# Three 16-head attentions: sums of the exponentials halved on GpSimd, two heads of each wave taken by ACT from PSUM

## The reference

```python
q = split_heads(queries @ Wq + bq)            # 8 x 16 x 128 x 8
k = split_heads(keys @ Wk + bk)
v = split_heads(values @ Wv + bv)
scores = jnp.einsum('bhqd,bhkd->bhqk', q, k) / jnp.sqrt(jnp.float32(HD))
scores = jnp.where(mask, jnp.float32(-1000000000000000.0), scores)
attn = jax.nn.softmax(scores, axis=-1)
ctx = jnp.einsum('bhqk,bhkd->bhqd', attn, v)
return ctx @ Wo + bo
```

## Time and profile before

| | us |
|---|---|
| median of 3 runs | 948.28 (948.22 to 954.27) |
| the profiled execution, span | 948.7 |
| PE busy | 882.5 (93%) |
| DVE busy | 670.6 (71%) |
| ACT busy | 556.3 (59%) |
| POOL busy | 182.2 (19%) |
| line 777 on DVE (128x512, PSUM and SBUF in), 192 times | 132.5, mean 690 ns |

### The profile page before, as it was taken

How to read it: one execution, slowest core, us unless ns; L and a number is a source line. 1 busy time by engine, 2 the same in 40 slices (tenths; PEclk the granted TensorE clock), 3 DMA queues, 4 the chain that set the end, 5 groups by cost and what they waited for, 6 DMA issues and landing times.

```text
span 948.7 us, 15321 instructions
## 1 busy us (share of the span) xinstructions
PE 882.5 (93%) x5199; PEld 572.2 (60%) x5219; DVE 670.6 (71%) x1123; ACT 556.3 (59%) x963; POOL 182.2 (19%) x157
## 2 busy tenths in 40 slices
PE   8999998999789888989899988999999999999997
PEld 4576645666535543445545554676446888888885
DVE  4566627777778849658858845542347999999996
ACT  5356624555655547366656541232476888888886
POOL 0111012332000000000020006335100443334430
PEclk9999999999999999999999999999999999999999
DMA  9000001111000000000000052401106999999982
GB/s 358 10 1 0 0 1 34 34 33 64 1 1 2 1 1 1 0 1 1 2 1 2 1 210 74 135 23 52 61 1 156 243 242 239 233 242 245 239 226 67
DMA packets 27746, 76.76 MB, mean 81 GB/s; under 512 B 4464, under 2 KB 10864, under 8 KB 27264
## 3 DMA queue, kind: packets, MB, share of 16 engines
q1 hardware_dynamic: 26448, 73.50, 28.2%
q0 software_dynamic: 1248, 2.57, 0.8%
HBM read 72.31 MB, written 5.27 MB: 82 GB/s over the span
## 4 chain that ended last, share of the span: by engine, by line
PE 69%; DVE 17%; ACT 9%; issue 3%; DMA 1%; SPq 0%; POOL 0%; DVEq 0%; another core or an unknown queue 0%; ACTq 0%; POOLq 0%
PE ps L743 9%; PE ps L745 9%; PE ps L744 9%; PE ps L1106 4%; PE ps L582 3%; PE ps L574 3%; PE ps L1122 2%; PE ps L599 2%; PE ps L593 2%; PE ps L280 2%; DVE arena L712 2%; PE ps L1386 2%; PE ps L217 2%; DVE arena L716 2%; DVE parts L777 2%
## 5 line engine op out<-in xcount | busy, mean ns | idle before, releaser
L743 PE MATMUL ps<-parts 128*128 128x512 f32 x416 | 169.0, 406 | 7.0 <-DVE parts L957 3.4
L745 PE MATMUL ps<-parts 128*128 128x512 f32 x416 | 162.3, 390 | 0.0
L744 PE MATMUL ps<-parts 128*128 128x512 f32 x416 | 162.2, 390 | 0.0
L773 ACT ACTIVATE parts<-ps 128x512 fp32r<-128x512 f32 x192 | 115.1, 600 | 61.2 <-PE ps L745 32.9
L777 DVE TENSOR_TENSOR parts<-ps,parts 128x512 fp32r<-128x512 f32 x192 | 132.5, 690 | 7.2 <-ACT parts L773 1.5
L2394 DVE TENSOR_TENSOR ps<-ps,arena 128x512 f32<-128x512 f32 x156 | 108.3, 694 | 3.6 <-DMA arena<-m_comb 2.5
L743 PEld LDWEIGHTS ps<-parts 128*128 128x128 f32 x416 | 78.2, 188 | 36.7 <-DVE parts L777 9.7
L1930 ACT ACTIVATE ps<-ps 128x512 f32<-128x512 f32 x156 | 90.8, 582 | 2.9 <-PE ps L745 0.4
L761 POOL TENSOR_TENSOR parts<-ring,zeros 128x1024 fp32r<-128x1024 f32 (+2 forms) x36 | 50.8, 1421 | 214.3 <-PE ps L745 177.3
L745 PEld LDWEIGHTS ps<-parts 128*128 128x128 f32 x416 | 78.1, 188 | 16.7
L744 PEld LDWEIGHTS ps<-parts 128*128 128x128 f32 x416 | 78.2, 188 | 15.2 <-issue 0.5
(11 more groups left out here) (447 smaller groups left out, 1402.0 us busy)
## 6 DMA issues: line engine op xcount, KB each, us to landing
arena<-m_comb SPq DMA_DIRECT2D x156, 256.0 KB, 5.6
ring<-m_in SPq DMA_DIRECT2D x20, 512.0 KB
arena<-m_in SPq DMA_DIRECT2D x4, 1408.0 KB
pack<-pack_in SPq DMA_DIRECT2D x1, 2058.5 KB, 10.2
ring<-m_up_in SPq DMA_DIRECT2D x8, 256.0 KB
slots_x<-empty_in SPq DMA_DIRECT2D x1, 1491.6 KB
pack<-pack_in SPq DMA_DIRECT2D x1, 1186.0 KB, 14.7
pack<-pack_in SPq DMA_DIRECT2D x1, 1149.5 KB, 12.3
```

Source lines behind the costliest of these rows:

```text
L743: nc.tensor.matmul(dst, w_high, x_high, start=start, stop=False, skip_group_check=True)
L744: nc.tensor.matmul(dst, w_high, x_low, start=False, stop=False, skip_group_check=True)
L745: return nc.tensor.matmul(dst, w_low, x_high, start=False, stop=stop, skip_group_check=True)
L773: nc.scalar.activation(m_hh[0:rows, p], ps[0:rows, src, :], ACT.Copy).then_inc(R(t, "_hh"), 1)
```

## The change

For the first seven elements the sums no longer come from PE. POOL adds the halves of each exponential row three times (128 columns to 64, 32 and 16) for six of the eight heads of a wave, DVE sums the 16 that are left, takes the reciprocals of the 16 sums of an element (one per query and head) and copies each to 8 columns; PE transposes that 128x128 tile (`turn_inverse`), ACT copies it to SBUF (`spread_inverse`), and DVE's `outputs` only multiplies. The last element keeps `total` and the reciprocal.

The other two heads of a wave (`DIRECT`) are not subtracted by DVE: ACT reads their scores from PSUM, with the negated maximum as bias, and gives their sums by `accum_out`. So the subtraction and the exponential in place cover 768 columns, and the scores of the next wave in the same banks wait for the exponentials. The scale 8^-0.5 moves to q: to the activation that adds q's bias (with the bias scaled ahead), and in f2 to the products with cosine and sine.

```diff
--- before.py
+++ after.py
@@ -28,6 +28,7 @@
 NH, HD = 16, 8
 ROWG = 4
 GH = NH // ROWG
+DIRECT = 2
 XH = 8
 E = 8
 NE, TOPK = 160, 8
@@ -326,8 +328,14 @@
         a_p = A(8192, 2, NH // 2, P)
         a_q = A(10240, T)
         a_k = A(11264, T)
-        a_mx = A(12288, 2, NH // 2)
+        a_nmx = A(12288, 2, NH // 2)
         a_rec = A(12304, 2, P)
+        a_sum = A(12560, 2, 2, NH // 2)
+        a_inv = A(20352, 2, P)
+        a_one = A(12592, NH)
+        a_half = A(20864, NH // 2 - DIRECT, HD * 8)
+        a_quarter = A(21376, NH // 2 - DIRECT, HD * 4)
+        a_eighth = A(21632, 2, 2, NH // 2 - DIRECT, HD * 2)
         a_v = A(12672, B, NH, 4 * HD)
         a_vflat = A(12672, B * NH * 4 * HD)
         a_rope = A(16768, 2, 2, 2, HALF)
...
@@ -496,8 +505,8 @@
 
         WAVES, UNITS = 2 * B, (E * 2 * M0_CH, NB)
         LEFT = {"a_kproj": 2, "a_qproj": 2, "a_q_ready": 2, "a_k_ready": 2, "a_kb0": GH, "a_kb1": GH, "a_vproj": 1, "a_v_ready": 1,
-                "a_scores": WAVES, "a_mx": WAVES, "a_z": WAVES, "a_p": WAVES, "a_turned": WAVES, 
-                "a_pt": WAVES, "a_weighed": B, "a_rec": B, "a_oT": B, "a_rope_k": 0, "a_rope_q": 0,
+                "a_scores": WAVES, "a_mx": WAVES, "a_z": WAVES, "a_p": 2 * WAVES, "a_turned": WAVES, 
+                "a_pt": WAVES, "a_added": 3 * (WAVES - 2), "a_weighed": B, "a_rec": B, "a_spread": B - 1, "a_oT": B, "a_rope_k": 0, "a_rope_q": 0,
                 "m_logits": 1, "m_lg": 1, "m_e": 1, "m_pad": (1, B + 1), "m_parts": (3, 4), "m_wturned": 1, "m_wT": 1, "m_spread": (2 * E, 2 + NB - SOON), "m_xw": (2 * E, NB),
                 "m_xwh": (2 * E, NB), "m_xwl": (2 * E, 2 + NB - SOON),
                 "m_xh": 2, "m_xl": 2, "m_wh": (2 * E, 2), "m_split": (E, 1),
@@ -576,7 +585,7 @@
                 ins.then_inc(R(t, "_scores"), 1)
 
             def turn(v, w):
-                wait("_p", w + 1)
+                wait("_p", 2 * w + 2)
                 wait("_pt", w)
                 for n in range(NH // 2):
                     ins = nc.tensor.transpose(ps[:, 4 + n // 4, (n % 4) * P:(n % 4 + 1) * P], a_p[:, v, n, :], ident)
...
@@ -600,6 +609,11 @@
                                  a_pt[:, b % 2, r * GH + n, :], start=(n == 0), stop=(n == GH - 1), skip_group_check=True,
                                  tile_position=(0, 32 * r))
                 ins.then_inc(R(t, "_weighed"), 1)
+
+            def turn_inverse(b):
+
+                wait("_rec", b + 1)
+                nc.tensor.transpose(ps[:, 6 + b % 2, P:2 * P], a_inv[:, b % 2, :], ident).then_inc(R(t, "_weighed"), 1)
 
             wait("_kb0", GH)
             if rope:
@@ -619,13 +633,16 @@
                         if b == 0 and v == 0:
                             fill(5, 4)
                         wait("_z", w + 1)
+                        wait("_p", 2 * w + 2)
                         scores(b + 1, v)
                     if b == 1 and v == 0:
                         wait("_v_ready", 1)
                         pe.wait_ge(S("filled"), 9)
-                    if b > 0:
-                        (total if v else weigh)(b - 1)
+                    if b > 0 and v == 0:
+                        weigh(b - 1)
                     turn(v, w)
+                    if b > 0 and v == 1:
+                        turn_inverse(b - 1)
             weigh(B - 1)
             total(B - 1)
             if not rope:
@@ -656,17 +673,29 @@
                                            bank(first + p).rearrange("p (n d) -> p n d", d=HD), ACT.Copy)
             ins.then_inc(R(t, "_v_ready"), 1)
 
-        def narrow_scalar(act, t, rope, scale, bq=None):
+        def narrow_scalar(act, t, rope, bq=None):
             wait = waits(act, t)
             credited_once(act, t, "_pt")
             if not rope:
                 for p in range(2):
                     wait("_qproj", p + 1)
-                    nc.scalar.activation(half(a_q, p), bank(2 + p), ACT.Identity, bias=bq).then_inc(R(t, "_q_ready"), 1)
+                    nc.scalar.activation(half(a_q, p), bank(2 + p), ACT.Identity, bias=bq, scale=SCALE8).then_inc(R(t, "_q_ready"), 1)
 
             def exps(v, w):
                 wait("_z", w + 1)
-                nc.scalar.activation(a_p[:, v], a_p[:, v], ACT.Exp, scale=scale).then_inc(R(t, "_p"), 1)
+                nc.scalar.activation(a_p[:, v, DIRECT:], a_p[:, v, DIRECT:], ACT.Exp).then_inc(R(t, "_p"), 1)
+                b = w // 2
+                if b >= 2:
+                    wait("_rec", b - 1)
+                for m in range(DIRECT):
+                    ins = nc.scalar.activation(a_p[:, v, m, :], ps[:, 2 * v, m * P:(m + 1) * P], ACT.Exp, bias=a_nmx[:, v, m:m + 1],
+                                               accum_out=a_sum[:, b % 2, v, m:m + 1])
+                ins.then_inc(R(t, "_p"), 1)
+
+            def spread_inverse(b):
+
+                wait("_weighed", b + 1)
+                nc.scalar.activation(a_rec[:, b % 2], ps[:, 6 + b % 2, P:2 * P], ACT.Copy).then_inc(R(t, "_spread"), 1)
 
             def copies(b, v, w):
                 wait("_turned", w + 1)
@@ -680,6 +709,8 @@
                     if w + 1 < WAVES:
                         exps(1 - v, w + 1)
                     copies(b, v, w)
+                if b > 0:
+                    spread_inverse(b - 1)
 
         ROPED = ((4, 6), (2, 4))
 
@@ -690,9 +721,10 @@
                 for k, (proj, part) in enumerate((("_kproj", "_rope_k"), ("_qproj", "_rope_q"))):
                     wait(proj, p + 1)
                     for m, tab in enumerate(("cos", "sin")):
-                        nc.vector.tensor_tensor(a_rope[:, k, m, p].rearrange("p (b t) -> p b t", b=HB),
-                                                bank(ROPED[p][k] + m).rearrange("p (b t) -> p b t", b=HB),
-                                                W(tab).unsqueeze(1).to_broadcast([P, HB, P]), ALU.mult).then_inc(R(t, part), 1)
+                        nc.vector.scalar_tensor_tensor(out=a_rope[:, k, m, p].rearrange("p (b t) -> p b t", b=HB),
+                                                       in0=bank(ROPED[p][k] + m).rearrange("p (b t) -> p b t", b=HB), scalar=SCALE8 if k else 1.0,
+                                                       in1=W(tab).unsqueeze(1).to_broadcast([P, HB, P]),
+                                                       op0=ALU.mult, op1=ALU.mult).then_inc(R(t, part), 1)
                     if p == 0:
                         restore_x(k)
 
@@ -703,23 +735,38 @@
                     waits(pool, t)(part, 2 * p + 2)
                     nc.gpsimd.tensor_tensor(half(dst, p), a_rope[:, k, 0, p], a_rope[:, k, 1, p], ALU.add).then_inc(R(t, ready), 1)
 
-        def narrow_vector(dve, t, meanwhile=None):
+        def narrow_vector(dve, t, link, meanwhile=None):
             wait = waits(dve, t)
 
             def maxima(v, w):
                 wait("_scores", w + 1)
                 sc = ps[:, 2 * v:2 * v + 2, :].rearrange("p a (g k) -> p (a g) k", g=4)
-                nc.vector.tensor_reduce(a_mx[:, v], sc, AX.X, ALU.max).then_inc(R(t, "_mx"), 1)
+                if w >= 2:
+                    wait("_p", 2 * w - 2)
+                nc.vector.tensor_reduce(a_nmx[:, v], sc, AX.X, ALU.max, negate=True).then_inc(R(t, "_mx"), 1)
                 wait("_mx", w + 1)
                 if w >= 2:
                     wait("_turned", w - 1)
-                nc.vector.tensor_tensor(a_p[:, v], sc, a_mx[:, v].unsqueeze(2).to_broadcast([P, NH // 2, P]),
-                                        ALU.subtract).then_inc(R(t, "_z"), 1)
+                    wait("_added", 3 * w - 5)
+                nc.vector.tensor_tensor(a_p[:, v, DIRECT:], sc[:, DIRECT:], a_nmx[:, v, DIRECT:].unsqueeze(2).to_broadcast([P, NH // 2 - DIRECT, P]),
+                                        ALU.add).then_inc(R(t, "_z"), 1)
+
+            def inverse(b):
+
+                wait("_added", 6 * b + 6)
+                wait("_p", 4 * b + 4)
+                link(nc.vector.tensor_reduce(a_sum[:, b % 2, :, DIRECT:], a_eighth[:, b % 2], AX.X, ALU.add))
+                link(nc.vector.reciprocal(a_one, a_sum[:, b % 2].rearrange("p v m -> p (v m)")))
+                nc.vector.tensor_copy(a_inv[:, b % 2].rearrange("p (h d) -> p h d", d=HD),
+                                      a_one.unsqueeze(2).to_broadcast([P, NH, HD])).then_inc(R(t, "_rec"), 1)
 
             def outputs(b):
                 wait("_weighed", b + 1)
-                nc.vector.reciprocal(a_rec[:, b % 2], ps[:, 6 + b % 2, P:2 * P]).then_inc(R(t, "_rec"), 1)
-                wait("_rec", b + 1)
+                if b < B - 1:
+                    wait("_spread", b + 1)
+                else:
+                    nc.vector.reciprocal(a_rec[:, b % 2], ps[:, 6 + b % 2, P:2 * P]).then_inc(R(t, "_rec"), 1)
+                    wait("_rec", b + 1)
                 nc.vector.tensor_tensor(a_oT[:, b * P:(b + 1) * P], ps[:, 6 + b % 2, 0:P], a_rec[:, b % 2],
                                         ALU.mult).then_inc(R(t, "_oT"), 1)
 
@@ -731,9 +778,27 @@
```

(25 more changed lines are left out.)

13 lines of the change are left out of this document (7 added, 6 removed).

## The result

The changed kernel takes **996.24 us** (median of 5 runs, 994.04 to 1004.46); the kernel before took 948.28 beside it (948.17 to 956.17). The ratio is 1.046 [1.041, 1.050], which is 43 us; the two medians alone lie 48 apart (1.051). Forecast were 975 with a range of 966 to 989: the side was right, the size was not. The forecast had 27 us to come.

A forecast was written before the change was run, and what follows sets the result against it. Attentions x1, x2, f2 were bound by PE's chain (f2, 7.04 us per element) and a ring over several engines (x2, 6.31). New stages 73.1, 66.9, 68.0 make 208.0 against 181.4, +26.6; with +0.3, 948.3 + 26.9 = 975, range 966 to 989.

The forecast's parts named there:

- the ring: Attentions, elements 2 to 7: DVE's multiply waits for ACT's spread, queued behind exponentials and copy; 8.1 us per element.
- the clock: PE's granted clock in the three attentions: expected not to fall below 1.00, so PE's new idle got no price.
- the tail: End of each attention, from the end of subtraction 14 to the last multiply: 13.3 us.
- The durations: Single instructions of the changed kernel on DVE, ACT and GpSimd, priced from rows of the earlier trace.
- the rope products: Between x2 and f2, eight products become scalar_tensor_tensor, 0.75 against 0.69 each: +0.3 us, bounds 0 and 0.6.
- GpSimd at nothing: GpSimd's halvings of the exponential rows, 2 us per wave, hidden because DVE needs them waves later: costed at nothing.
- rival 1: DVE's spread copy waits for GpSimd's halving, 1.0 per element on 18 periods: 990 to 993; chance 0.08.
- rival 2: PE's clock falls in the idle that the change opens; x2 alone +2.5 x 7: 985 to 993; chance 0.05.
- work of 3 us stands before every gap: Reason given for the low chance, 0.05, of PE's clock falling in its new idle of 1.6 to 2.2 us.
- about what the fill of the pipeline takes now: Elements 0 and 1: scores wait for exponentials from PSUM; 5.0 us from a subtraction's end, 5.5 with mask.
- Rivals 3 and 4: 3: a ring through PE decides, 952, chance 0.06; 4: no ring closes, larger sum of work decides, 928, chance 0.04.

The follow-up runs named there:

- the kernel with the clock held: Changed kernel plus products with zeros on PE from element 2 on, none added behind the last of them, and a longer fill before the first wave: 979.62 us, ratio 1.027.
- the first experiment: Changed kernel plus products with zeros on PE behind each first wave's transposes and behind the transposed inverses: 988.21 us, ratio 1.041.

## Why the prediction was wrong: right on the ring, wrong on the clock

**The ring: right.** Forecast was a period of 8.1 in x2 and f2; undisturbed passes take 8.10 and 8.14. The multiply was to start 2.70 after the subtraction, and does after 2.79 of idle. Moving that one instruction takes the loss away (0.997), moving the spread ahead of the copy takes 0.9 from the period, and putting a spread into the kernel before makes the loss appear. Each of the three was an edit of one place. With the clock held, the stages sum to 210.7 against 208.0 forecast. Of the 2.7 between them 1.6 lie in the tail of f2: from the end of subtraction 14 it takes 14.87 where 13.3 was forecast; the tails of x1 and x2 take 13.72 and 13.28. The subtraction of wave 4 ends at 14.69, 13.25 and 14.30 (x1, x2, f2) where 14.5, 13.1 and 14.2 were forecast.

**The durations: right.** Subtraction of 768 columns 0.96 (forecast 0.95), sum 0.34 (0.34), reciprocal 0.25 (0.24), exponential of 768 0.84 (0.85), the direct exponential 0.35 apart (0.35, from 256 columns of the earlier trace rows), spread 0.27 (0.27), GpSimd 0.99, 0.59 and 0.39 (1.0, 0.6 and 0.4, from the earlier trace rows). One small price was wrong: the rope products were to cost 0.3 and cost nothing (684 ns each before, 685 after). The stretch from x2 to f2 grew by 0.25 in this profiled execution, which looks like a hit and is luck: ten of the eleven experiments that have the same products take 16.12 or 16.13 there, as the kernel before does.

**GpSimd at nothing: right.** Its 2.0 us a wave lie beside other work, and DVE's waits never end on it in the changed kernel. The copy takes 0.23 there and never meets an addition of GpSimd, so rival 1 did not come. PE's share in f2 came to 81% (58.38 of 72.47) instead of nearly 75, in part because it worked at a lower clock.

**The clock: the step that failed.** The prediction gave rival 2 a chance of 0.05, with the words "work of 3 us stands before every gap", and the sum took PE's new idle, 1.6 to 2.2 us in each pass, at no price. The trace has the clock at 0.63 right after such work and a gap of 1.51, and at 0.79 over the whole of x2. The rival was also framed too narrowly in two ways. It was priced for x2 alone, while f2, with less idle, fell to 0.91 and x1 to 0.83. And it was set against the ring, where it comes **on top** of it, and can feed itself: slower transposes make the copy late, the copy makes the spread late, DVE's multiply waits up to 5.0 us instead of 2.8, and PE idles again behind DVE.

The rival looked for the idle in the ring alone, and more than half of the price lies outside it. Against the kernel with the clock held, 4.6 of the 18.4 lie ahead of the end of subtraction 4, 7.9 in the five passes from there to subtraction 14, and 5.8 in the tails. In x2, for which the rival had 2.5 a pass, the five passes cost 1.1 together and the start 3.8. There PE waits for the first direct exponentials, a wait that the prediction did see ("about what the fill of the pipeline takes now") and gave no clock. PE in the changed kernel, from its timeline and as a window (columns as above, PE alone):

```profile
448.91 1.13 PE L583 MATMUL ps<-arena 32*128 32x512 f32 x4 [2.08 <-ACT arena L691]
```
```profile
444.98:462.07 17.09, 15.01 (x81) 0.70 0.00 1
```

What the clock is worth stands in two comparisons. Inside the stages it is 18.4 (229.1 against 210.7, one profiled execution each). Between medians it is 16.6 (996.24 against 979.62), or by the ratios, 1.046 against 1.027, some 18. The ring's share is 29 by the stages. By the ratios alone the loss is 43, some 25 of it the ring's and 18 the clock's; between the medians it is 48. That the stages' 29 and 18 add up to about 48 is not a proof of either figure: the profiled execution of the changed kernel is 8.2 above its median, so its 18.4 may be too high. The other 6 us of that execution, +3.0 before x1 and +3.2 between x1 and x2, are not the change's doing: the first experiment's kernel has the whole change and begins x1 at 271.58 and x2 85.73 after x1, as before.

Under the Trainium skill's page TensorE: Matmul & The Clock Gate, section "A second HAM failure mode: psum-queue depth-cycling", brief idle times between groups of products, frequent enough, made the clock of another kernel go back and forth. The trace agrees in kind: in f2, with a gap of 1.4 to 1.5 us in most passes, the clock is 1.00 from 555.60 to 563.70, where PE is busy 6.42 of 8.10 us, and 0.63 from 567 to 571.

**How it could have been seen.** The earlier trace rows held one window at 1.00 with PE busy for just over half of it, and one at 0.68 after 2.25 of idle. The argument took the first for the case at hand. The rows did not settle whether gaps that return in every pass act like one gap, and the range should have held the price of being wrong on that: the prediction's own 2.5 a pass at most, 17.5 a stage, over three stages instead of one gives up to 1027, and half of it 1001. That 996 was measured would still have agreed with it by luck, since more than half of the price lay at the starts and in the tails.

**Rivals 3 and 4** did not come: the spread is the last to end in every pass, and no stage gained.

## What to carry to other kernels

A short step that moves to another engine costs what stands **ahead of it in that engine's queue**. Ask whether that work waits for something queued behind the instruction that will wait for the step. If so, a ring is closed however idle the engine looks, and the cure is to move the consumer behind the independent work on its own engine (some 47 us here). Making one part of the ring shorter gave back less: the spread ahead of the copy left a ratio of 1.021. Idle that a new wait opens on PE has a price of its own, at the start and in the tail of a stage as well as in each pass. The granted clock of 1.00 in all three stages of the kernel before gave no warning, its 0.68 after idle elsewhere did; the range has to hold it. Products with zeros hold the clock, and pay where PE idles anyway (18.4 of stage time here); placed ahead of scores that are due as well, they gave 8.8 of that back.
